# Attention kernel: another order of score tiles, key tiles of scores and key tiles of sums on TensorE

## The reference

```python
B, L, D = x.shape                        # 4, 1024, 128; 16 heads of 8
qkv = (x @ w_qkv).reshape(B, L, 3, H, Dh)
...
attn = jnp.einsum('bhid,bhjd->bhij', q, k) * scale
attn = attn + phi_bias(L)[None, None]
attn = jax.nn.softmax(attn, axis=-1)
out = jnp.einsum('bhij,bhjd->bhid', attn, v)
...
x = x + 0.5 * ffn(layernorm(x)); x = x + attn(layernorm(x)); x = x + 0.5 * ffn(layernorm(x))
```

## Time and profile before

| | |
|---|---|
| median of 3 runs | 1120.49 us (1118.1 to 1120.71) |
| the profiled execution | 1122.93 us, its span 1121.1 us |
| TensorE (PE) busy in the span | 980.0 us, 87% |
| VectorE (DVE) busy | 911.8 us, 81% |
| ScalarE (ACT) busy | 726.9 us, 65% |
| GpSimd (POOL) busy | 358.1 us, 32% |
| mean granted TensorE clock | 0.947 of full speed |

### The profile page before, as it was taken

The page is one execution under the profiler, slowest core; times in us unless marked ns, Lnnn a source line. Parts: engine busy times, 40 slices in busy tenths (PEclk is TensorE's granted clock), DMA queues, the critical chain, the costliest instruction groups (busy, mean ns, idle before and its releaser), DMA issues. The chain is left out here.

```text
span 1121.1 us, 36169 instructions
## 1 busy us (share of the span) xinstructions
PE 980.0 (87%) x11663; PEld 548.3 (49%) x11667; DVE 911.8 (81%) x1801; ACT 726.9 (65%) x1573; POOL 358.1 (32%) x468
## 2 busy tenths in 40 slices
PE   5529998574999999999999999999999998639996
PEld 4429998340333333333333333333333346639996
DVE  6447886547999999999999999999999976548885
ACT  1114443470888888888888888888888884224443
POOL 1623444003232323232332323232333323524343
PEclk9999999695899999999999999999999997569998
DMA  9612221686122222222222222222222444622220
GB/s 305 239 63 67 67 66 35 171 278 171 51 72 72 69 69 60 75 73 60 74 64 71 72 64 69 69 69 69 61 76 71 103 106 171 236 71 71 63 67 26
DMA packets 84957, 106.70 MB, mean 95 GB/s; under 512 B 15835, under 2 KB 68065, under 8 KB 84368
## 3 DMA queue, kind: packets, MB, share of 16 engines
q1 hardware_dynamic: 79344, 93.51, 28.7%
q0 software_dynamic: 5568, 12.63, 3.2%
HBM read 74.14 MB, written 36.55 MB: 99 GB/s over the span
## 5 line engine op out<-in xcount | busy, mean ns | idle before, releaser
L1126 DVE TENSOR_REDUCE nmax<-psS 128x1 f32<-128x1024 f32 x512 | 600.7, 1217 | 39.1 <-PE psS L979 31.5
L1269 ACT ACTIVATE big<-psE 128x512 f32<-128x512 f32 x1024 | 553.0, 598 | 101.5 <-PE psE L964 98.9
L964 PE MATMUL psE<-qop,kop 122*32 122x512 bf16 x4096 | 319.0, 386 | 4.5 <-ACT big L1269 3.0
L1341 POOL TENSOR_TENSOR big<-big,const 128x512 f32<-128x512 f32 x128 | 162.7, 1271 | 443.2 <-ACT big L1269 443.2
L997 PE MATMUL psV<-big,vst 128*9 128x256 f32 x4096 | 265.9, 379 | 1.3
L979 PE MATMUL psS<-maxop 32*128 32x512 bf16 x1024 | 176.7, 395 | 28.3 <-DVE nmax L1126 13.3
L997 PEld LDWEIGHTS psV<-big,vst 128*9 128x9 f32 x4096 | 101.4, 90 | 115.7 <-issue 12.4
L964 PEld LDWEIGHTS psE<-qop,kop 122*32 122x32 bf16 x4096 | 90.7, 96 | 132.0 <-ACT big L1269 59.7
L979 PEld LDWEIGHTS psS<-maxop 32*128 32x128 bf16 x1024 | 48.0, 91 | 188.7 <-issue 114.6
L733 ACT ACTIVATE siga<-psGa,w1sa 128x128 f32<-128x128 f32 x156 | 44.6, 368 | 61.0 <-PE psGa L645 61.0
L733 ACT ACTIVATE sigb<-psGb,w1sb 128x128 f32<-128x128 f32 x156 | 44.6, 368 | 60.7 <-PE psGb L645 60.7
(11 more groups left out here) (190 smaller groups left out, 924.9 us busy)
## 6 DMA issues: line engine op xcount, KB each, us to landing
maxop<-qk_parts SPq DMA_DIRECT2D x256, 64.0 KB, 1.9
qop<-qk_parts SPq DMA_DIRECT2D x64, 144.0 KB
kop<-qk_parts SPq DMA_DIRECT2D x64, 144.0 KB
weighted_sums<-osum SPq DMA_DIRECT2D x64, 128.0 KB
qk_parts<-part SPq DMA_DIRECT2D x16, 384.0 KB, 3.6
xsa<-sorted_a SPq DMA_DIRECT2D x39, 128.5 KB, 2.1
xsb<-sorted_b SPq DMA_DIRECT2D x39, 128.5 KB
w1a<-in_w SPq DMA_DIRECT2D x1, 4128.0 KB
```

The costliest lines, as they stand in the source:

```text
L964: last = nc.tensor.matmul(psE[BANK[turn]][32 * c:32 * c + 32, :], kop[b][0:TROWS, lo:lo + 32], qop[b][0:TROWS, half * HALF:(half + 1) * HALF],
L1126: nc.vector.tensor_reduce(nmax[r % 2][:, qt:qt + 1], psS[n % 2][:], AX.XY, ALU.max, negate=True).then_inc(s_max, 1)
L1269: nc.scalar.activation(prob[r % 2][:, lo:lo + HALF], psE[BANK[16 * (r % NBUF) + n]][:], ACT.Exp).then_inc(s_exp, 1)
L1341: nc.gpsimd.tensor_tensor(dst, dst, diag[:, 4 * h:4 * h + 4, :], ALU.mult).then_inc(s_diag, 1)
```

## The change

In each quarter of a step TensorE's order becomes another. Before: key tile 2p of scores, S tiles 2p and 2p+1, key tile 2p+1 of scores, two key tiles of sums. Now: S tile 2p, both key tiles of scores, S tile 2p+1, both key tiles of sums. `gather` takes a key tile instead of a quarter, with the same waits ahead of the same key tiles (0 and 4). The numbers of matmuls, the banks, the semaphores and the programs of the other engines stay.

```diff
-                def gather(p):
-
-                    if p == 0:
+                def gather(k):
+
+                    if k == 0:
                         pe.wait_ge(s_vst, i)
                         if r % 2 == 1 and later(at, -1, 1):
                             pe.wait_ge(s_ev, 2 * q + (r - 1) // 2)
-                    if p in (0, 2):
-                        pe.wait_ge(s_diag, 2 * i - 1 + p // 2)
-                        pe.wait_ge(s_exp, 16 * i - 8 + 8 * (p // 2))
+                    if k in (0, 4):
+                        pe.wait_ge(s_diag, 2 * i - 1 + k // 4)
+                        pe.wait_ge(s_exp, 16 * i - 8 + 8 * (k // 4))
                     side = (r + 1) % 2 * QUART
-                    for k in (2 * p, 2 * p + 1):
-                        for c in range(4):
-                            at_c = k * PBLK + c * QUART
-                            last = nc.tensor.matmul(
-                                psV[32 * c:32 * c + VW, side:side + QUART], vst[(r + 1) % 2][:, k, :],
-                                prob[(r + 1) % 2][:, at_c:at_c + QUART], start=(k == 0), stop=(k == KT - 1))
-                    if p == 3:
+                    for c in range(4):
+                        at_c = k * PBLK + c * QUART
+                        last = nc.tensor.matmul(
+                            psV[32 * c:32 * c + VW, side:side + QUART], vst[(r + 1) % 2][:, k, :],
+                            prob[(r + 1) % 2][:, at_c:at_c + QUART], start=(k == 0), stop=(k == KT - 1))
+                    if k == KT - 1:
                         last.then_inc(s_pv, 1)
 
                 for p in range(4):
+                    if live(at, 2):
+                        score(2 * p)
                     if live(at, 0):
                         weigh(2 * p)
-                    if live(at, 2):
-                        score(2 * p)
-                        score(2 * p + 1)
                     if live(at, 0):
                         weigh(2 * p + 1)
+                    if live(at, 2):
+                        score(2 * p + 1)
                     if live(at, -1):
-                        gather(p)
+                        gather(2 * p)
+                    if live(at, -1):
+                        gather(2 * p + 1)
                     if at is not None:
                         between(at, p)
```

## The result

| | before | changed |
|---|---|---|
| median | 1119.81 us (4 runs, 1118.1 to 1120.71) | 1257.25 us (4 runs, 1254.99 to 1258.87) |
| ratio | | 1.1228, 95% interval 1.1203 to 1.1253 |
| span of the profiled execution | 1121.1 us | 1257.0 us |

The changed kernel is 12.3% slower, 137 us. Forecast were 1248 us and a range of 1224 to 1278. The median before rests on one run more than the 1120.49 from which the prediction reckons.

A forecast was written before the change was run, and what follows sets the result against it. No engine alone was the bound, but how TensorE's order lets them overlap. 61 steps x 4 quarters x 3.02 us plus 7.5 gives 744.4 against 617.1, +127: median about 1248 us, range 1224 to 1278.

The forecast's parts named there:

- The fourth W tile waits for the first exponential: TensorE, each quarter: with three banks the fourth W starts 1.09 us after the first instead of 0.66, standing 0.43.
- the exception: Last W tile of a four-head turn takes the bank of two tiles before: 0.50 us more, 15 times, 7.5 us.
- Changes between S and V cost as much as those between S and W: TensorE, each quarter: S to V and V to S taken at 0.32 us each, within bounds of 0.22 and 0.32.
- Rival 1: TensorE's changes next to V cost nothing: quarter 2.82 us, 49 us less, 1199; chance 0.05.
- The sum: Steps 1 to 61: four quarters of 3.02 us each, plus 7.5, is 744.4 us against 617.1, +127 us.
- Costs put at nothing: VectorE's maxima, the `psV` copy, GpSimd and SyncE's rows for W tiles, and operand loads: each no added time.
- The copy of `psV`: ScalarE, odd steps: after the first exponential, it delays the quarter's second to fourth, not the one awaited; cost nothing.
- Rival 2: In each quarter the fourth W tile doesn't wait: 2.59 us a quarter, +15 us, 1135 to 1143; chance 0.01.
- Rival 3: In the loop, evenly fed VectorE becomes the only bound, its 36.8 us of idle time goes: faster, 1084; chance 0.02.
- Rival 4: TensorE's clock falls in the loop: 1690 us if it lasted throughout, 1336 for a fifth of the time; chance 0.03.

The follow-up runs named there:

- the first expectation: Changed kernel with S tile, key tile of scores, key tile of sums, twice a quarter; about 1142 us expected, 1181.18 us measured, 1.0525 to the kernel before.
- S, S, W, W, V, V, copy first: Changed kernel with both S tiles of a quarter side by side, and ScalarE's copy of `psV` ahead of an odd step's first exponential; 1181.34 us, 1.0535 to before.
- S, S, W, W, V, V: Changed kernel with both S tiles of a quarter side by side, the four W tiles still in one piece; 1191.41 us, 1.0622 to the kernel before.

## Why the prediction was right, point by point

- **The fourth W tile waits for the first exponential.** Forecast 1.09 us from first to fourth, from steps 62 and 63; found 1.10. It waits in all 244 quarters, mostly with the same 0.27 in brackets. The run with four banks takes 111 us off the changed kernel. Since V then comes early enough to meet the copy, the wait's whole share is larger: in the stretch 753.3 - 633.6 = 120 us with the copy out of the way, 8.5 of them the exception.
- **Changes between S and V cost as much as those between S and W.** Forecast 0.32 each, the end of the bounds that was taken; found 0.32 (S to V) and 0.33 (V to S). Rival 1, which had them free, falls, and its reason with it. In the kernel before, the weight load of the first V after a W starts 0.21 us ahead of its matmul; in the changed one, after an S, it starts 0.002 us ahead. The loads of S start 0.004 to 0.005 ahead in either kernel. The Trainium skill, page "TensorEngine Tiling (Array Packing)", section Key Properties, says that a change of tiling mode drains TensorE. These numbers agree with it; that it is the shape of the tiles and no other difference between S and the rest was not tried by itself.
- **The sum.** 3.02 a quarter was forecast, 12.21 / 4 = 3.053 found: 244 x 0.033 = 8 us, nearly all of the difference between 1248 and 1257. Three terms were a hundredth short each: W to S and V to S measured 0.33 instead of 0.32, the first to the fourth W 1.10 instead of 1.09. The exception was 0.57 instead of 0.50 a turn, +1 us. Step 1 began 2 us earlier than before (287.40 against 289.42), where 0 to 1 us later had been forecast; the clock granted from 277.6 to 289.4 us was 0.64 there against 0.52 before. That the new S tiles cost 0.32 on either side already held the loss of the neighbour. But the 0.10 between the two S tiles of the old order in the earlier trace rows was a wait for a maximum and not work.
- **Costs put at nothing.** VectorE, GpSimd, SyncE and the loads stayed hidden: over the stretch the matmuls of S waited for a maximum for 0.6 us in all. VectorE waited for S once a quarter (256 times), not twice as forecast, and its share was 80% where 78 was forecast, ScalarE's 69% where 72 was. The copy of `psV` cost nothing in the changed kernel, as said, but the reason given was only half of it: it doesn't delay the fourth W, and V is late enough (1.75 after the first W) that the copy is done just before. That the two came out a hundredth apart is luck. With V earlier the copy costs 1.3 us in an odd step (11.72 against 10.40), which is why the first expectation missed by 39 us.
- **Rival 2**, no wait of the fourth W, was not what happened; four banks made it so, at 1146, and 1133 with the copy moved (16.5 us in the stretch; the rival had +15). **Rival 3**, faster through even feeding of VectorE: the S tiles were spread as it says, but with four changes TensorE's quarter never got under 2.59. **Rival 4**: the clock stayed at 1.00 through the loop, although TensorE stopped in every quarter.
- **How the two causes add up.** Over steps 1 to 61 the order alone costs 16.5 us, four W tiles in one piece with S in pairs 58, both together 136. They aren't additive, because the order before had a gap. Its quarter in most steps was 2.50 us, of which TensorE stood 0.32 between two S tiles, waiting for a maximum; the rest, 2.18, is its own pieces. Splitting the pairs adds 0.42 of work: 0.20 for the two changes more, and 0.22 for the second S tile, which now takes a place of its own instead of running beside the first. The wait for a maximum is gone for it, so a quarter is 2.60. In a quarter, in us:

| | TensorE's own pieces | stands | quarter |
|---|---|---|---|
| before | 2.18 | 0.32, S for a maximum | 2.50 |
| changed order, four banks, copy first | 2.60 | 0 | 2.60 |
| S, S, W, W, V, V, copy first | 2.18 | 0.45, W for a bank; 0.10, S for a maximum | 2.73 |
| changed | 2.60 | 0.45, W for a bank | 3.05 |

What comes in first fills the gap, and only what comes on top costs in full.

## What to carry to other kernels

With n buffers between two engines in lockstep, a run of n+1 products in one piece makes the producer wait for the consumer's whole latency (here 0.44 + 0.60 + 0.05), even when both have plenty of time on average; keep runs no longer than the buffers, and put other work between them. Spacing one stream evenly wasn't worth the changes of the array's shape here: count them in each period of an order, at 0.10 us each, and count the small tiles that ran side by side and no longer do, at 0.22 us each. And when work moves forward in an order, look for waits that its old place was hiding, such as the copy here; the stretch in which a pipeline runs down can show the new pattern before it is built, as steps 62 and 63 did.

## What the runs showed of the hardware

- A change between work in column groups (128 rows by 32 columns) and in row groups (32 rows by 128 columns) costs TensorE 0.10 to 0.12 us in either direction, with fp32 (V) as with bf16 (W).
- Two S tiles in different row groups, issued one behind the other, start 0.01 us apart and take the time of one (701.55, 0.40 us for four matmuls, in S, S, W, W, V, V). The same tile by itself takes a place of 0.22 beside the changes.
- V starts 0.22 to 0.23 us after the end of the copy it waits for (602.69 to 602.91), where a W tile starts 0.05 after the exponential. V's first key tile carries several waits; that these make the difference was not tried.
- The profile named GpSimd as what V waited for, whose instruction ended 0.05 us after ScalarE's copy. Moving the copy showed that the copy was it, and V then started before GpSimd's instruction had ended: of two releasers that end close together the inferred one can be the wrong one.
